# Two-layer attention at the end of a graph network: the last layer's neighbour sums made row tile by row tile instead of transposed

## The reference

```python
def _gat_layer(x, W, adj):
    proj = x @ W                            # 1354 x 512
    Wh, Ws = jnp.split(proj, 2, axis=-1)    # 1354 x 256 each
    scores = Wh @ Ws.T                      # 1354 x 1354
    a = jax.nn.softmax(scores, axis=-1) * adj
    out = a @ Wh
    out = out + x
    return jax.nn.leaky_relu(out, 0.01)
# x = _layernorm(x + _gat_layer(_gat_layer(x, W[0], adj), W[1], adj))
```

## Time and profile before

| | us |
|---|---|
| median of 3 runs | 515.81 (514.64 to 516.01) |
| profiled execution, its own time | 513.07 |
| its span | 511.3 |
| last TensorE instruction ends | 498.6 |
| TensorE busy | 482.5 (94%) |
| VectorE busy | 345.6 (68%) |
| ScalarE busy | 244.9 (48%) |
| GpSimd busy | 172.8 (34%) |

### The profile page before, as it was taken

One profiled execution on the slowest core, in us unless ns is written; L12 is line 12 of the kernel. 1 busy time (PEld: TensorE's weight loads), 2 busy tenths in 40 slices (PEclk: granted clock), 3 DMA queues, 4 the chain that ended last, 5 costly groups with the idle time before them and its releaser, 6 DMA issues.

```text
span 511.3 us, 5688 instructions
## 1 busy us (share of the span) xinstructions
PE 482.5 (94%) x1901; PEld 304.3 (60%) x1901; DVE 345.6 (68%) x747; ACT 244.9 (48%) x450; POOL 172.8 (34%) x175
## 2 busy tenths in 40 slices
PE   5999999999999989999999999999999999999890
PEld 4899755455555778876545446555556545554580
DVE  4789879999862879475237647935623794576776
ACT  5767369974885543333335424424324664342300
POOL 1422423542332068632004414502310462424511
PEclk9999999999999999999999999999999999999895
DMA  9856300000543000000000000000000000000101
GB/s 308 242 176 187 108 2 0 0 0 9 210 159 91 1 1 0 1 1 1 0 0 1 0 1 0 2 0 0 1 0 0 1 1 2 0 0 0 42 21 47
DMA packets 8148, 20.68 MB, mean 40 GB/s; under 512 B 976, under 2 KB 4708, under 8 KB 8120
## 3 DMA queue, kind: packets, MB, share of 16 engines
q1 hardware_dynamic: 6840, 18.75, 11.1%
q0 software_dynamic: 464, 0.79, 0.8%
q10 hardware_dynamic: 816, 0.79, 0.5%
HBM read 18.94 MB, written 1.39 MB: 40 GB/s over the span
## 4 chain that ended last, share of the span: by engine, by line
PE 82%; DVE 8%; ACT 3%; issue 3%; POOL 2%; DMA 1%; POOLq 0%; ACTq 0%; DVEq 0%
PE psum L1457 18%; PE psum L1504 15%; PE psum L1239 10%; PE psum L1275 9%; PE psum L1335 5%; PE psum L1222 4%; PE psum L1437 4%; PE psum L1575 3%; PE psum L1294 2%; PE psum L1410 2%; PE psum L1539 2%; PE psum L1156 2%; PE psum L1321 1%; PE psum L1389 1%; PE psum L1486 1%
## 5 line engine op out<-in xcount | busy, mean ns | idle before, releaser
L1457 PE MATMUL psum<-QT,xT 128*128 128x512 f32 (+3 forms) x264 | 107.7, 543 | 0.3 <-DVE xT L1027 0.3
L1504 PE MATMUL psum<-ST,Wh 128*128 128x512 f32 (+3 forms) x220 | 94.9, 563 | 1.6 <-DVE vbuf L1009 1.1
L410 POOL TENSOR_TENSOR es<-es,ST 128x512 f32<-128x512 f32 (+3 forms) x60 | 72.3, 1204 | 59.2 <-ACT ST L613 57.5
L600 ACT ACTIVATE ST<-psum 128x512 f32<-128x512 f32 (+3 forms) x66 | 36.0, 546 | 86.2 <-DVE rm L960 80.9
L1457 PEld LDWEIGHTS psum<-QT,xT 128*128 128x128 f32 (+1 forms) x264 | 48.2, 186 | 47.2 <-issue 40.7
L960 DVE TENSOR_TENSOR rm<-psum,rm 128x512 f32<-128x512 f32 (+3 forms) x60 | 37.3, 622 | 46.8 <-PE psum L1457 46.8
L1504 PEld LDWEIGHTS psum<-ST,Wh 128*128 128x128 f32 (+1 forms) x220 | 40.8, 190 | 40.4 <-issue 33.2
L360 POOL TENSOR_TENSOR rstd<-veps,nhalf 128x1 f32<-128x1 f32 (+1 forms) x44 | 29.3, 667 | 95.0 <-DVE veps L767 94.9
L1275 PE MATMUL psum<-eb,x_all 128*128 128x512 f32 (+3 forms) x132 | 52.8, 545 | 0.0
L982 DVE TENSOR_TENSOR ST<-ST,psum 128x512 f32<-128x512 f32 (+3 forms) x66 | 39.9, 614 | 17.6 <-PE psum L1486 17.6
L613 ACT ACTIVATE ST<-ST 128x512 f32<-128x512 f32 (+3 forms) x66 | 37.8, 579 | 27.6 <-DVE ST L982 25.0
(11 more groups left out here) (165 smaller groups left out, 757.0 us busy)
## 6 DMA issues: line engine op xcount, KB each, us to landing
adj_rows<-in_adj_dram SPq DMA_DIRECT2D x10, 677.0 KB, 5.0
rows<-in_adj_dram SPq DMA_DIRECT2D x10, 677.0 KB, 4.1
out_dram<-xs SPq DMA_DIRECT2D x10, 128.0 KB, 1.7
x_all<-in_x_dram SPq DMA_DIRECT2D x2, 512.0 KB, 6.7
W<-in_L_gnn_W_stack_dram SPq DMA_DIRECT2D x2, 512.0 KB, 5.6
adj_rows<-in_adj_dram SPq DMA_DIRECT2D x1, 338.5 KB
rows<-in_adj_dram SPq DMA_DIRECT2D x1, 338.5 KB
w0n<-in_L_gnn_weight_dram ACTq DMA_DIRECT2D x1, 256.0 KB, 5.1
```

The lines of the kernel that those rows point to most:

```text
L410: nc.gpsimd.tensor_tensor(es[0:r, g % 2, 0:w], es[0:r, g % 2, 0:w], buf(g)[0:r, j, 0:w], ALU.add)\
L600: nc.scalar.activation(buf(g)[0:r, j, 0:w], psum[0:r, SB[n % 3], 0:w], ACT.Copy).then_inc(st_ready.sem, 1)
L1457: last = nc.tensor.matmul(psum[0:r, SB[n % 3], 0:w], xT[l][:, k, j * P:j * P + r], QT[:, k, c0:c1], start=(k == 0), stop=(k == KD - 1))
L1504: last = nc.tensor.matmul(bank(AB[g] + m, 0, w), Wh[g // NC][0:r, j, m * P:(m + 1) * P], buf(g)[0:r, j, 0:w], start=(j == 0), stop=(j == T ...
```

## The change

All three chunks of the second layer are summed as chunk 5 was, in natural layout, one row tile after another. `sum_n(i, j0, j1)` takes the place of `sum_t(3)`, `sum_t(4)` and `sum_last`: for output tile i it runs over the source tiles j0 to j1, into bank 2 or 3 in turn. `turn_y`, `finish_y`, and the spreading of the denominators of chunks 3 and 4 (`den_diag`, `spread_rden`, `rdb_evac`) are gone, `scale_t`, `add_t`, `leaky_t` of these chunks too. `turn_x1` and `x1_copy` are made for all 11 tiles instead of 3, during the score tiles of chunk 4. `finish_n` finishes all 11 tiles; `FIN4` and `FIN5` set after which step of chunk 4 and chunk 5 tiles 0 to 6 are finished, and tiles 7 to 10 follow. `s_tile(5, .)` is spread between the sums of tiles 0 to 2.

```diff
-    FIN = {5: 0, 7: 1, 9: 2, 10: 3}
+    XB = [3, 5, 2]
+    FIN4 = {1: 0, 5: 1, 8: 2}
+    FIN5 = {1: 3, 5: 4, 8: 5, 10: 6}
```

GpSimd's order:

```diff
+            for j in range(T):
+                add_probs(4, j)
+                if j - 2 in FIN4:
+                    rsqrt(NG, FIN4[j - 2])
+            for j in range(T):
+                add_probs(5, j)
+                if j in FIN5:
+                    rsqrt(NG, FIN5[j])
```

VectorE: the new `finish_n` (its other instructions are those of before) and the order:

```diff
+            def finish_n(i):
+                r, g = kk(i), NC + (i * P) // BANK
+                n = i - tiles(g)[0]
...
+                if n == 0:
+                    rden_cols(g)
+                    dve.wait_ge(rden_ready.sem, g + 1)
+                dve.wait_ge(x1n_ready.sem, i + 1)
+                dve.wait_ge(sum_done.sem, NC + i + 1)
+                nc.vector.scalar_tensor_tensor(out=v, in0=psum[0:r, 2 + i % 2, 0:D], scalar=rden[0:r, g, n:n + 1],
+                                               in1=x1n(i)[0:r, :], op0=ALU.mult, op1=ALU.add).then_inc(gat_read.sem, 1)
...
             max_reduce(4)
+            run_max(5, 0)
+            run_max(5, 1)
             soft_step(4, 0)
             soft_step(4, 1)
             for s in range(T):
+                if s + 2 < T:
+                    run_max(5, s + 2)
+                soft_step(4, s + 2)
+                if s == T - 3:
+                    max_reduce(5)
+                if s in FIN4:
+                    finish_n(FIN4[s])
+                if s - 1 in FIN4:
+                    finish_out(FIN4[s - 1])
             for s in range(T + 2):
                 soft_step(5, s)
-                if s in FIN:
-                    finish_y(FIN[s])
-                if s - 1 in FIN:
-                    finish_out(FIN[s - 1])
+                if s in FIN5:
+                    finish_n(FIN5[s])
+                if s - 1 in FIN5:
+                    finish_out(FIN5[s - 1])
```

TensorE: the new sum and the order, which replaces all calls of `sum_t(3)`, `sum_t(4)`, `sum_last`, `turn_y` and `spread_rden` of these chunks:

```diff
+            def sum_n(i, j0, j1):
+                r, g = kk(i), NC + (i * P) // BANK
+                n = i - tiles(g)[0]
+                if j0 == 0:
+                    pe.wait_ge(gat_read.sem, NC + max(i - 1, 0))
+                if i <= 1:
+                    pe.wait_ge(x1n_ready.sem, T - 2 + i)
+                for j in range(j0, j1):
+                    q = kk(j)
+                    if n == 0:
+                        pe.wait_ge(pt_ready.sem, g * T + j + 1)
+                    last = nc.tensor.matmul(psum[0:r, 2 + i % 2, 0:D], buf(g)[0:q, j, n * P:n * P + r], Wh[1][0:q, j, :],
                                             start=(j == 0), stop=(j == T - 1))
...
             for j in range(T):
                 s_tile(4, j)
-                if j == 1:
+                if j == 0:
                     wh1(T - 1)
-                if j in (5, 7, 9):
-                    turn_x1(CROSS + (j - 5) // 2)
+                else:
+                    turn_x1(j - 1)
+            turn_x1(T - 1)
+            sum_n(0, 0, 2)
             max_turn(4)
+            s_tile(5, 0)
+            sum_n(0, 2, 5)
             max_spread(4)
+            s_tile(5, 1)
+            sum_n(0, 5, 8)
+            s_tile(5, 2)
+            sum_n(0, 8, T)
+            s_tile(5, 3)
             den(3)
+            for i in (1, 2):
+                for n in range(4):
+                    sum_n(i, 3 * n, min(3 * n + 3, T))
+                    if 4 * i + n < T:
+                        s_tile(5, 4 * i + n)
+            sum_n(3, 0, 3)
             max_turn(5)
+            sum_n(3, 3, 8)
             max_spread(5)
+            sum_n(3, 8, T)
+            for i in range(EB, CROSS):
+                sum_n(i, 0, T)
+                if i == EB:
+                    den(4)
+            sum_n(CROSS, 0, 8)
+            den(5)
+            sum_n(CROSS, 8, T)
+            for i in range(CROSS + 1, T):
+                sum_n(i, 0, T)
```

More of the change, by code:

```diff
@@ L411, in add_probs @@
                         .then_inc(es_added.sem, 1)
-            for g in range(G - 1):
+            for g in range(NC + 1):
                 for j in range(T):
@@ L701, in _ @@
                 both(3, s)
-                if s == 1:
+                if s == 0:
                     wh1_evac(T - 1)
-                if s in (5, 7, 9):
-                    x1_copy(CROSS + (s - 5) // 2)
+                else:
+                    x1_copy(s - 1)
+            x1_copy(T - 1)
             max_diag(4)
+            st_copy(5, 0)
+            st_copy(5, 1)
             exp_probs(4, 0)
@@ L709, in _ @@
             for s in range(T):
[L710 to L714, removed]
+                if s + 2 < T:
+                    st_copy(5, s + 2)
+                    exp_probs(4, s + 2)
+                if s == T - 3:
+                    max_diag(5)
             for j in range(T):
                 exp_probs(5, j)
-            den_diag(4)
-            rdb_evac(4)
         @block.vector
@@ L1002, in scale_t @@
                 t = sums_of(g)
[L1003 to L1005 removed]
+                if g >= 1:
                     dve.wait_ge(xT1_ready.sem, g)
@@ L1106, in _ @@
             for s in range(T):
[L1107 to L1113, removed]
+                if s + 2 < T:
+                    run_max(5, s + 2)
+                soft_step(4, s + 2)
+                if s == T - 3:
+                    max_reduce(5)
[3 more added lines that the diff above has]
+                    finish_out(FIN4[s - 1])
             for s in range(T + 2):
                 soft_step(5, s)
-                if s in FIN:
-                    finish_y(FIN[s])
-                if s - 1 in FIN:
-                    finish_out(FIN[s - 1])
[L1120 to L1126, removed]
-                    finish_out(i - 1)
[L1128 to L1131, removed]
-            for i in range(CROSS, T):
-                if i + 1 < T:
-                    finish_n(i + 1)
-                finish_out(i)
+                if s in FIN5:
+                    finish_n(FIN5[s])
+                if s - 1 in FIN5:
+                    finish_out(FIN5[s - 1])
+            first = len(FIN4) + len(FIN5)
+            for i in range(first, T):
+                finish_n(i)
+                if i > first:
+                    finish_out(i - 1)
+            finish_out(T - 1)
         @block.tensor
```

134 lines of the change are left out of this document (32 added, 102 removed).

## The result

The changed kernel's median is 502.06 us (502.01 to 503.84, 4 runs) against 515.91 us (514.64 to 517.45, 4 runs) before: ratio 0.9749, 95% interval 0.9714 to 0.9785. That is faster, by 13.9 us in this comparison. Two later comparisons, each beside runs of the kernel before on one chip, gave 0.9779 (0.9734 to 0.9824) and 0.9796 (0.9762 to 0.9831), that is 12.4 and 11.1 us.

The account below looks back on a forecast made before the run. TensorE was taken to set the pace up to 498.6 us, then VectorE, GpSimd and the output transfer. 12.7 us saved less 2.9 of new waits gave -9.8, from 515.81 to 506.0 us, range 502.0 to 510.5.

Parts of the forecast that it names:

- TensorE's path without new waits: TensorE from 399.9 us to its last product: 8.8 us gone, 1.76 added, so that product ends 7.05 us earlier.
- the slow records: 12 TensorE records after the 2.17 us wait, at 0.376 instead of 0.216 us each; removing the excess saves 1.9 us.
- The tail: Last product to the span's end: only tile 10 left to finish, 7.1 us instead of 12.7, 5.6 less.
- The eight transposes at their full 1.76 us: Eight added `turn_x1` on TensorE from 399.9 us, 0.22 us each, costing 1.76 us and not more.
- The 14.2 us of cover: Tiles 5 to 7, 3 x 4.75 us, stand before chunk 5's first product and cover its soft steps.
- VectorE through with chunk 4: VectorE ends chunk 4 at 458.5 us: 453.4 without waits, plus 2 for scores and maxima, 3 for GpSimd.
- The pauses before tiles 6, 7 and 8: New TensorE waits for VectorE's `finish_n` to read the bank: 1.3, 1.3 and 0.2 us, sum 2.8 to 2.9.
- the wait for GpSimd in chunk 5: VectorE instructions with two SBUF inputs held by GpSimd's additions: 0.6 to 1 us per tile in chunk 5.
- the clock's rival: TensorE's clock falls at tile 6's wait and stays down: 17.6 us lost against 9.8 gained, 523.6 us, chance 0.03.
- The first rival: VectorE keeps up with TensorE's tiles, so the whole 12.7 us gain stays: 503.1 us, chance 0.25.
- The median: Whole kernel's time: the 9.8 us gain set against the median of 515.81 us gives 506.0 us.
- the 2.17 us wait: TensorE's wait at 477.9 us, attributed to chunk 5's soft steps; forecast gone, saving 2.17 us.

Follow-up runs that it names:

- e_joint5: Changed kernel with chunk 5's three row tiles summed together again, source tile by source tile, in banks 0, 1 and 4; ratio 0.9891 to the kernel before.
- e_fin_late: Changed kernel with tile 4 finished two soft steps later and tile 5 one later; ratio 0.9836 to the kernel before.
- e_no_adds: Changed kernel with GpSimd's additions for chunks 4 and 5 of the second layer cut to one column; ratio 0.9763 to the kernel before.
- e_before_cover: Kernel before, with chunk 3's denominators spread after score tile 10 of chunk 5 instead of in front of it; ratio 0.9973.
- e_banks3_b: Changed kernel with three PSUM banks instead of two for the row tiles' sums, run again in more rounds; 500.58 us, ratio 0.9733 to the kernel before.
- e_before_split: Kernel before, with tiles 8 and 9 summed first and tile 10 after, without the bank 7 wait; `turn_y(4)` to `turn_y(7)` moved too; ratio 0.9974.

## Why the prediction was right

- **TensorE's path without new waits.** Forecast: end 7.05 us earlier. Measured in the stretch: TensorE's last product ends at 494.9 - 400.98 = 93.9 against 99.75, 5.8 us earlier, and 1.5 us of pauses are in that: 7.3. Right. One term was a little too large: the sum took the slow records at 1.9 us, and start to start they cost 4.35 - 12 x 0.216 = 1.8.
- **The tail.** Forecast 7.1 us, measured 7.05, so 5.65 less than before. e_joint5 shows 4.2 us of the 5.65 directly.
- **The eight transposes at their full 1.76 us, nothing from `x1_copy`, no wait at `max_spread(4)`.** Right: the windows show TensorE busy for all of 400.98 to 457.14. The 14.2 us of cover in front of chunk 5's first product were enough too: no pause stands there.
- **VectorE through with chunk 4.** Forecast 458.5, that is 59.65 us into the stretch. Its last product with the adjacency of chunk 4 ends at 460.6 - 400.98 = 59.6. Right, with the 3 us of waits for GpSimd: L991, L1042 and L1043 are 3.2 us above bare there.
- **The pauses before tiles 6, 7 and 8** were in the right places and too large: 1.3, 1.3 and 0.2 forecast, 0.42, 0.55 and none measured. The mis-sized term is the wait for GpSimd in chunk 5. I laid 2.4, 1.1 and 0.8 us; measured are 1.5, 0.6 and 0.5 (lengths above bare in the changed kernel's timeline). The pauses cost 1.5 us start to start where 2.85 were forecast; these 1.35 us, and 0.25 in TensorE's path without them, are the 1.6 us by which the traces' gain, 11.4, exceeds the forecast 9.8. The granted clock stayed at 1.00 through these pauses, which answers the clock's rival; in e_fin_late it fell after one of 2.66 us, for 1.7 us and not for the rest of the kernel. The first rival, that VectorE keeps up, was held to be weak because three soft steps and a tile take 4.97 us even without waits; e_no_adds shows that this excess alone makes no pause, so GpSimd's additions decided it.
- **The median.** Forecast 506.0, measured 502.06, only 0.06 us above the lower end of the range. Beyond the stretch's 1.6 us, 2.4 us lie ahead of the change, where the two programs are the same, and this part is luck, not forecast: the later comparisons gave 12.4 and 11.1 us instead of 13.9. The stretch begins at 398.85 us in the profile of the kernel before, the earliest of all, and in the others between 398.95 and 403.70. Nearly all of this comes in two places. At 166 us the changed kernel and e_before_cover are already 2.0 to 2.1 us late, the others 0.3 at most; why stays open. And from 170 to 190 us the granted clock is 1.00 in the kernel before, the changed kernel and e_banks3_b, 0.91 in eight profiles and 0.83 in two (e_before_cover, e_joint5), which costs 1.3 to 1.6 us and 2.9 us.
- **What the sum hid.** It priced the 2.17 us wait and the slow records at 4.1 us of TensorE's path. As a part of this change TensorE's path agrees with that, and as a price by itself it is wrong: e_before_split took them out without shortening the chain behind them and gained 0.8. Nor was it the soft steps as such that TensorE waited for, but bank 7 with the maxima, which tile 10's sum was to take over. VectorE's chain, with the turns that TensorE makes for it, was within about 2 us of TensorE's (an estimate, above), and the change gained since it shortened both: VectorE's by the scaling, adding and turning back of whole chunks, TensorE's by the waits, the turns and the spreading.

## What to carry to other kernels

When one engine's wait is priced, look at what the others still have to do behind it: in the kernel before, TensorE's longest wait, with the slow records behind it, was 3.4 us of its path and moved the end by 0.8 us. The 11.4 us came from shortening both chains: 5.8 us at TensorE's last product, and 5.65 us because only one tile is left to finish after it. Here VectorE and TensorE handed tiles over through two PSUM banks at almost equal pace, and TensorE paused at two of the tiles; a third bank took both pauses away (1.3 to 1.4 us), while finishing the tiles earlier in VectorE's list moved the loss to a later place.

## What the runs showed of the hardware

- An operation on VectorE that reads the same SBUF tensor twice (L1042) is held by GpSimd's addition like one that reads two tensors: 1.05 and 1.17 us for tiles 0 and 1 of the changed kernel, 0.42 with the additions at one column. The Trainium skill's page SBUF — State Buffer, section Who interferes with whom, states it for two SBUF inputs, and e_no_adds agrees.
- Pauses of TensorE of 0.42, 0.55 and 1.20 us left the granted clock at 1.00. Those of 2.17 us (two profiles) and 2.66 us were followed by 3.8 to 5.25 us at a granted clock of 0.50 to 0.61, and after the same pause of 2.17 us 12 records took 4.35 us start to start in one profile and 5.25 in another.
- A long pause is not the only thing that the clock fell after. Near 175 us, in the part that all kernels share, the granted clock fell in ten of thirteen profiles with no pause over 0.2 us just before. In e_before_cover TensorE was busy for all of 160 to 176 us, and the clock was 1.00 to 174 us and 0.50 from 176 to 180. The same products in the kernel before, at a granted clock of 1.00:

```profile
173.07 0.80 PE L1275 MATMUL psum<-eb,x_all 74*128 74x330 f32 x2
...
174.12 1.13 PE L1321 MATMUL psum<-Wsa,hT 128*128 128x256 f32 x4 [0.17 <-ACT hT L525]
```

and in e_before_cover:

```profile
175.04 1.45 PE L1275 MATMUL psum<-eb,x_all 74*128 74x330 f32 x2
...
176.48 2.06 PE L1321 MATMUL psum<-Wsa,hT 128*128 128x256 f32 x4
```
